# Graph attention with a routed feed-forward: output weights centred on chip, the second norm's variance from ScalarE, and side work dealt over the steps of a block

## The reference, cut

```python
def gnn(x, adj, Wq, bq, Wk, bk, Wv, bv, Wo, bo, gamma, beta):  # x: 8 x 1024 x 128, 4 heads of 32
    ...
    scores = clip(q @ k.T / sqrt(32), -10, 10)
    scores = where(adj == 0, -10, scores)
    attn = softmax(scores)             # for each chunk of 128 keys by itself
    out = sum_of_chunks(attn @ v) @ Wo.T + bo + x
    mu, var = mean(out), mean(square(out - mean(out)))
    return (out - mu) * rsqrt(var + 1e-5) * gamma + beta
def ffn(x, Wg, bg, W1, b1, W2, b2):     # 8 experts, hidden 256, the two best of each token
    mask = one_hot(top_k(x @ Wg + bg, 2)).sum()
    return sum_e(mask_e * (gelu(x @ W1_e + b1_e) @ W2_e + b2_e))
x = x + gnn(layernorm(x), adj, ...)     # layernorm has neither weight nor bias
x = x + ffn(layernorm(x), ...)
```

## Time and profile before

| | us |
|---|---|
| median of 3 runs | 757.75 (757.08 to 758.26) |
| span of the profiled execution | 773.1 |
| first clip of the loop / first clip of block 15 / last clip, by the trace | 17.08 / 504.8 / 541.95 |
| first clip of block 3 / of block 14 | 116.41 / 471.64 |
| clips of steps 2 and 3 of block 14 | 479.89, 484.11 |
| clips of steps 2 and 3 of block 15 | 514.68, 519.95 |
| TensorE / VectorE / ScalarE / GpSimd busy, of the span | 91% / 81% / 64% / 76% |

### The profile page before, as it was taken

How to read it: one execution, slowest core, us unless ns; L and a number is a source line. 1 busy time by engine, 2 the same in 40 slices (tenths; PEclk the granted TensorE clock), 3 DMA queues, 4 the chain that set the end, 5 groups by cost and what they waited for, 6 DMA issues and landing times. The chain is left out here.

```text
span 773.1 us, 17066 instructions
## 1 busy us (share of the span) xinstructions
PE 699.8 (91%) x5416; PEld 365.5 (47%) x5416; DVE 624.5 (81%) x1455; ACT 496.4 (64%) x898; POOL 584.0 (76%) x689
## 2 busy tenths in 40 slices
PE   4898999999999999999999999787979789999994
PEld 2222323333333333333333333231668679999994
DVE  4699899999999999999999999999677445545552
ACT  4656567777677775777767776544775346666663
POOL 7579495989879898798987988969476555667664
PEclk9999999999999999999999999997989789999998
DMA  7620000001010010100100001041322223333330
GB/s 272 212 65 28 12 18 14 28 29 56 15 43 28 29 56 15 43 28 29 56 15 29 29 15 43 15 138 42 88 68 75 81 81 94 88 86 98 100 90 1
DMA packets 47958, 45.42 MB, mean 59 GB/s; under 512 B 6981, under 2 KB 42576, under 8 KB 47872
## 3 DMA queue, kind: packets, MB, share of 16 engines
q1 hardware_dynamic: 41888, 31.60, 14.2%
q0 software_dynamic: 5984, 12.74, 4.5%
HBM read 27.73 MB, written 18.34 MB: 60 GB/s over the span
## 5 line engine op out<-in xcount | busy, mean ns | idle before, releaser
L744 ACT ACTIVATE e<-e 128x2048 f32<-128x2048 f32 x128 | 244.5, 1910 | 139.5 <-DVE e L946 132.6
L946 DVE SCALAR_TENSOR_TENSOR e<-scores_ps,bound_mem 128x2048 f32<-128x2048 f32 x128 | 292.2, 2283 | 25.6 <-PE scores_ps L436 23.8
L829 ACT ACTIVATE e<-scores_ps,bound_mem 128x128 f32<-128x128 f32 x364 | 104.4, 374 | 59.9 <-PE scores_ps L604 51.9
L1417 POOL DMA_INDIRECT out<-e,near x91 | 91.3, 1003 | 65.5 <-POOL near L1410 28.3
L455 PE MATMUL z_ps<-e,one_column 128*32 128x512 f32 x1024 | 136.0, 603 | 0.0
L1390 POOL TENSOR_TENSOR ctx_part<-ctx_part,z_inv 128x1024 f32<-128x1024 f32 x60 | 115.0, 1917 | 23.3 <-DVE z_inv L962 22.7
L1402 POOL TENSOR_TENSOR ctx_sum<-ctx_sum,ctx_part 128x512 f32<-128x512 f32 x90 | 115.8, 1287 | 6.0
L604 PE MATMUL scores_ps<-e,bound_mem 128*128 128x128 f32 x728 | 101.9, 284 | 8.7 <-ACT e L829 3.5
L604 PEld LDWEIGHTS scores_ps<-e,bound_mem 128*128 128x128 f32 x728 | 92.4, 198 | 12.0 <-issue 7.2
L954 DVE STREAM_TRANSPOSE ctx_part<-ctx_ps 128x512 f32<-128x512 f32 x128 | 90.3, 705 | 1.4 <-PE ctx_ps L448 1.3
L1364 POOL DMA_INDIRECT sorted_rows<-x_rows,slot x64 | 63.6, 994 | 27.2 <-issue 17.7
(11 more groups left out here) (171 smaller groups left out, 1032.1 us busy)
## 6 DMA issues: line engine op xcount, KB each, us to landing
near<-sorted_rows SPq DMA_DIRECT2D x91, 130.0 KB
near<-in_x SPq DMA_DIRECT2D x16, 256.0 KB, 2.7
bound_mem<-in_adjT SPq DMA_DIRECT2D x4, 1024.0 KB, 9.1
x_post<-in_x SPq DMA_DIRECT2D x16, 256.0 KB, 2.7
sorted_rows<-pad_row SPq DMA_DIRECT2D x1, 3640.0 KB, 14.7
out<-e,near POOLq DMA_INDIRECT x91
sorted_rows<-x_rows,slot POOLq DMA_INDIRECT x64
bound_mem<-in_w SPq DMA_DIRECT2D x1, 1024.0 KB
```

Source lines behind the costliest of these rows:

```text
L744: nc.scalar.activation(every, every, ACT.Exp, scale=SCORE_SCALE).then_inc(exp_done, 1)
L829: nc.scalar.activation(e_flat[:, h_at:h_at + P], scores_ps[:, i % 2, k * P:(k + 1) * P], ACT.Gelu, bias=part_flat[:, bias_at:bias_at + 1]) ...
L946: dve.scalar_tensor_tensor(out=e[:, s % E_RING], in0=scores_ps[:], scalar=-CLIP, in1=to, op0=ALU.max, op1=ALU.min).then_inc(clipped, 1)
L1417: nc.gpsimd.indirect_dma_start(out=out_rows, out_offset=bass.IndirectOffsetOnAxis(ap=near_u[:, id_at:id_at + 1], axis=0), in_=e_flat[:, at ...
```

## The change

The output weights are centred along the output features on chip: TensorE multiplies `Wo` by `centre` = I - 1/128, ScalarE copies the product to `wo_centred`, and the bias is centred likewise. The normalised x has mean zero already, so the projected sum has mean zero, and its variance is the mean of its squares. `statistics(ln["2"])` leaves VectorE, and `root(ln["2"])` GpSimd. Instead ScalarE squares the bank in `square_proj` with a sum as a second output, GpSimd makes the inverse root in `root_proj`, and ScalarE scales in `normalise_proj`. The projection is split in two halves over steps 1 and 2. `choose` is cut in three (`find_best`, `find_places`, `mark_pair`) for steps 2, 3 and 4, and the first norm's statistics begin with one tile in step 1. `mark_pair` writes its code to `job_ps[1]` for blocks under 11, after the wait for `n2_ready`. The wait of `turn_xn` on `one_hot_ready` becomes one on `gate_drained`. `normalise_x2` goes from step 6 to step 7, ahead of `drain_q`; GpSimd's `add_residual` goes ahead of `scale(u - 1, 4)`.

```diff
             def turn_xn(v):
-                need(pe, one_hot_ready, done(v - 5))
+                need(pe, gate_drained, done(v - 5))
...
-                    ins = pe.matmul(job_ps[1][:, cols], ctxT[:, cols], w_proj[:, W_O, :], start=False, stop=True,
+                    ins = pe.matmul(job_ps[1][:, cols], ctxT[:, cols], wo_centred[:], start=False, stop=True,
...
-            pe.matmul(job_ps[1][:, 0:1], w_proj[:, W_O, :], bv_sb[:], start=True, stop=True).then_inc(bias_filled, 1)
+            pe.wait_ge(centre_ready, 1)
+            pe.matmul(z_ps[:, 0:D], w_proj[:, W_O, :], centre[:], start=True, stop=True).then_inc(wo_filled, 1)
+            pe.wait_ge(wo_ready, 1)
+            pe.wait_ge(bv_ready, 1)
+            pe.matmul(z_ps[:, D:D + 1], wo_centred[:], bv_all[:], start=True, stop=False)
+            pe.matmul(z_ps[:, D:D + 1], centre[:], bo_sb[:], start=False, stop=True).then_inc(bias_filled, 1)
...
-                    if u < LATE and j == 2 and is_block(u - 2):
-                        project(u - 2)
-                    if u >= LATE and j in (1, 2):
+                    if j in (1, 2) and is_block(u - 2):
                         project(u - 2, range(2 * j - 2, 2 * j))
...
+            def square_proj(v):
+                need(act, x2_ready, v)
+                need(act, var2_ready, v)
+                act.wait_ge(proj_filled, v + 1)
+                for t in range(TILES):
+                    ins = nc.scalar.activation(n2[:, t, :], proj_rows[:, t, :], ACT.Square, scale=1.0 / float(np.sqrt(D)),
+                                               accum_out=mean_square[:, t, :])
+                ins.then_inc(squared, 1)
+
             def normalise_proj(v):
-                need(act, x2_ready, v)
-                normalise(ln["2"], v, n2, job_ps[1][:].rearrange("p (t d) -> p t d", d=D))
+                act.wait_ge(rstd2_ready, v + 1)
+                for t in range(TILES):
+                    ins = nc.scalar.activation(n2[:, t, :], proj_rows[:, t, :], ACT.Copy, scale=rstd2[:, t, :])
+                ins.then_inc(n2_ready, 1)
...
+            nc.scalar.activation(bv_all[:], bv_sb[:], ACT.Copy, scale=float(CHUNKS)).then_inc(bv_ready, 1)
+            act.wait_ge(wo_filled, 1)
+            nc.scalar.activation(wo_centred[:], z_ps[:, 0:D], ACT.Copy).then_inc(wo_ready, 1)
             normalise_x(0)
+            act.wait_ge(bias_filled, 1)
+            nc.scalar.activation(bo_all[:], z_ps[:, D:D + 1], ACT.Copy).then_inc(bias_ready, 1)
...
+                    if j == (7 if u < LATE else 6) and is_block(u - 2):
+                        normalise_x2(u - 2)
                     if j == 7 and u > 0 and is_block(u + 2):
                         drain_q(u + 2)
-                    if j == 6 and is_block(u - 2):
-                        normalise_x2(u - 2)
...
+            def mark_pair(v):
                 dve.wait_ge(best_at_ready, v + 1)
-                code = job_ps[0][:, 2 * P:2 * P + TILES].rearrange("p (t a) -> p t a", a=1)
+                if code_ps(v) is job_ps[1]:
+                    dve.wait_ge(n2_ready, v + 2)
+                code = code_ps(v)[:, 2 * P:2 * P + TILES].rearrange("p (t a) -> p t a", a=1)
...
+            def root_proj(v):
+                pool.wait_ge(squared, v + 1)
+                nc.gpsimd.tensor_scalar(var2[:], mean_square[:], 1.0, LN_EPS, ALU.mult, ALU.add).then_inc(var2_ready, 1)
+                pool.wait_ge(var2_ready, v + 1)
+                need(pool, n2_ready, v)
+                nc.gpsimd.tensor_tensor(rstd2[:], var2[:], minus_half[:, 0:TILES], ALU.pow).then_inc(rstd2_ready, 1)
...
-                if u >= LATE:
-                    root(ln["2"], u - 2)
+                if is_block(u - 2):
+                    root_proj(u - 2)
...
-                if k == 3:
-                    dve.wait_ge(proj_filled, 15)
-                    statistics(ln["2"], 14, proj_rows)
...
-                if k == 13:
-                    dve.wait_ge(proj_filled, 16)
-                    statistics(ln["2"], 15, proj_rows)
```

More of the change, by code:

```diff
@@ L519, in rank @@
                 if rank_ps(v) is job_ps[1]:
-                    need(pe, ln["2"]["s_out"], done(v if v == 13 else v + 1))
+                    need(pe, n2_ready, done(v if v == 13 else v + 1))
                 to = rank_ps(v)[:, 0:(TILES + 1) * NP].rearrange("p (t n) -> p t n", n=NP)
@@ L1010, in choose @@
                                   code_table[:].to_broadcast([P, TILES, NP]), ALU.is_equal).then_inc(one_hot_ready, 1)
+            def choose(v):
+                find_best(v)
+                find_places(v)
+                mark_pair(v)
             def place(v):
@@ new lines, in _ @@
+                    if u < LATE and is_block(u - 3):
+                        if j == 2:
+                            find_best(u - 3)
+                        if j == 3:
+                            find_places(u - 3)
+                        if j == 4:
+                            mark_pair(u - 3)
+                    if u >= LATE and j == (3 if u == LATE else 0):
+                        choose(u - 3)
+                    if j == 4 and is_block(u + 3):
+                        begin_statistics_x(u + 3, range(1 if u else 0, TILES))
@@ L1184, in _ @@
+                    if j == 5 and is_block(u - 2):
+                        begin_statistics_x2(u - 2)
+                        if u >= LATE:
+                            end_statistics(ln["3"], u - 2)
+                    if j == 6 and is_block(u + 3):
                         end_statistics(ln["1"], u + 3)
-                    if j == (6 if u < LATE else 5) and is_block(u - 2):
-                        dve.wait_ge(x2_ready, u - 1)
-                        statistics(ln["3"], u - 2, x_rows[:, (u - 2) % 3, :, D:2 * D])
+                    if j == 6 and u < LATE and is_block(u - 2):
+                        end_statistics(ln["3"], u - 2)
```

114 lines of the change are left out of this document (61 added, 53 removed).

## The result

The changed kernel takes 749.06 us (median of 4 runs, 746.87 to 752.06) where the kernel before, run beside it, takes 758.0 (757.08 to 759.22): a ratio of 0.9878, 95% interval 0.9854 to 0.9902. The forecast was 748.0 with a range of 743.5 to 756.

What follows compares the result with a forecast made beforehand. TensorE and VectorE, both nearly full, were taken to hold each other up in turn. Inner blocks -9.0, block 14 -0.3, block 15 -1.3, start +0.4, slots +0.5 gave -9.7: 748.0 us, range 743.5 to 756.

Steps and rivals of the forecast that it cites:

- What bounds the block: Inner block of 32.27 us: TensorE and VectorE alternate, heavy in different steps, so a block costs more than the fuller needs.
- The inner blocks: Blocks 3 to 13: longest of loop, VectorE and TensorE per step gives 31.45 against 32.27, 9.0 us in 11 blocks.
- step 0: Inner blocks: TensorE's turn waits for the normalisation moved behind step 7's exponential, losing 0.22 us, for 3.84.
- The squares: ScalarE, second norm: free up to 0.49 us each, beyond that 0.1 costs 0.4 a block; 0.42 assumed.
- (a): Squares cost 0.5 to 0.7 each, mark_pair holds step 5's clip; at 0.6 total 754; 0.17 shared with the slots rival.
- (b): Squares of 0.85 by a read-out emptying ScalarE each time: blocks 33.0, total 765, slower than before; chance 0.07.
- The start: Before the main loop: centring delays the first clip from 17.08 to 18.3, mostly hidden, +0.4 us (0.2 to 1.3).
- Blocks 14 and 15: Last blocks lose statistics in step 2: -0.3 and -1.3 us; step 4 of block 15 may move 2 us either way.
- After the last clip: Slots: VectorE loses two statistics of 1.4 us, ScalarE gains squares; +0.5 us, from -3 to +4.
- Rival (c): Slots, paced by ScalarE, give the gain back by +4 to +7: 752 to 755; 0.17 shared with (a).
- Rival (d): More gain: no turn_xn2 wait, block 15's port waits gone, half-clock stretches shrink: 743 to 746; chance 0.10.
- Carrying the microseconds over: Sum made in a profiled execution of 773.1 us, applied unscaled to the median of 757.75, giving 748.0.

Runs made afterwards that it cites:

- spare work in steps 7 and 3: The change plus four unread VectorE statistics a block in blocks 3 to 13: in step 7 748.13 us (blocks 31.40), in step 3 753.67 us (31.70).
- the deal: The kernel before with side work spread over steps as in the change, second norm's statistics left on VectorE: 768.47 us, ratio 1.0121.
- the norm without the deal: The change with projection and choose whole in step 2 again, keeping centred weights and squares on ScalarE: 752.89 us, ratio 0.9932.
- effective 0.75: The change with ScalarE's four squares and sums taken three times, extras unread: 765.1 us against 755.62 for the kernel before beside it.
- the second set: The change, unedited, run and profiled again beside other kernels on the same chip: 746.53 us, ratio 0.9852 to the kernel before.

## Why the prediction was right, point by point

**What bounds the block.** Right. The two engines held each other up in turn, and the statement that a block cost more than its fuller engine needs is what the change cashed in: TensorE's idle time went from 0.98 us a block to 0.19 (0.35 predicted). The spare work in steps 7 and 3 shows the same from the other side: free in one, 0.29 us in the other.

**The inner blocks.** Predicted 3.84, 4.67, 3.66, 3.62, 4.06, 3.62, 7.98, together 31.45; measured 3.71, 4.63, 3.74, 3.63, 4.06, 3.62, 8.00, together 31.39, where 9.0 us of gain were predicted and 9.9 came (355.23 to 345.35). The largest miss is step 0: the turn on TensorE was to lose 0.22 us waiting for the moved normalisation. It starts at 247.09, right behind the end of the normalisation at 247.04, and the row sums ahead of it end at 246.96: it waits about 0.1. The deal of step 2 into steps 3 and 4, and the keys that show in step 4, came as worked out. The same reckoning gave 32.11 and 33.0 for the norm and the deal done apart, and 32.12 and 33.02 were measured.

**The squares.** The threshold was right (0.49 predicted, 0.46 to 0.47 measured), and its slope too. Their price was not: 0.42 was taken, 0.25 measured. The bound of 0.46 rested on reading out the sum as an operation of its own, which it is, with 0.19 us near the 0.21 of the smallest activation. But it overlaps the activation before it and the one behind it, so that the pair takes no longer than one gelu does with its bias. By the page on activations (the Trainium skill, ScalarE: Activation LUTs, What ACT_TABLE_LOAD costs) the activation alone was 0.29; the row has 0.26. Since both prices lie under the threshold, the error cost the forecast nothing; it only made the rivals (a) and (b), with 0.5 to 0.7 and 0.85 as a price, look nearer than they were. Their blocks, at 0.6 and 0.85, were also a little off by the prediction's own slope, which gives 31.89 and 32.89 for 32.0 and 33.0. At an effective 0.75 a block takes 32.55, where the prediction's slope gives 31.45 + 4 (0.75 - 0.49) = 32.49, and the kernel does come out slower than before, so the mechanism of (b) is real.

**The start.** This is the term that was mis-sized: "+0.4 (0.2 to 1.3)". The part ahead of the first clip was as said, 17.08 to 18.21 where 18.3 was predicted, and as said it is mostly hidden: the norm without the deal has it too and reaches block 2 at 85.64. What was left out is another edit of the same diff: VectorE ends the statistics of block u + 3 in step 6 instead of 5, and in block 0 GpSimd stands in its queue for just that, with the bounds of block 1 behind it. That costs 1.0 us in step 7 of block 0, and taking this one line back gives it back. Block 1 is longer too, 33.27 and 33.26 before against 33.6 at the least with the change's start, and the granted clock falls there whenever the bound comes late. Both were put at nothing. Together they are 1.3 us or more, set by the order. With the line taken back the clock stays up, but block 1 takes 33.83, so what is left of its length isn't settled. A late load and a clock fallen in block 0 come on top, in kernels with and without the change alike: 85.3 to 87.4 before and 85.3 to 90.5 after at block 2. One profiled execution of each could not have told the true cost of the start to a microsecond.

**Blocks 14 and 15.** -0.3 and -1.3 predicted; -0.7 and -1.4 measured against the first execution. Step 2 of block 15 got 1.7 us shorter (5.27 to 3.56) where 1.39 were counted, and step 4 0.5 longer (8.86 to 9.37).

**After the last clip.** +0.5 (-3 to +4) predicted; 213.3 before, 212.9 and 213.7 after. Rival (c) did not come: statistics off VectorE and squares onto ScalarE leave the length as it was; that the two cancel is likely, but no run parts them. Rival (d), 743 to 746, was nearly reached in the second set, 746.53, with 0.9 us more from the inner blocks and more from the last ones than the forecast had. Of (d)'s three causes the wait of `turn_xn2` did come out smaller (0.1 us), and the second execution had no half-clock stretch in block 0, but step 4 of block 15 grew instead of shrinking.

**Carrying the microseconds over.** The sum was made in an execution 15 us longer than the median, and taken over unscaled. That came out right, for the excess lay behind the last clip (231.2 against 213.3) and not in the loop whose blocks were counted. The prediction gave no such reason, so this was in part luck. In that execution the granted clock was 0.85 between 575 and 633 us and 0.95 from there to the end; why it fell there isn't known. The whole was helped by luck too: the forecast of -9.7 met -8.9 because the inner blocks and the last ones gave 1.4 us more than counted and the start took more back.

## What to carry to other kernels

When two engines hand the bound back and forth, add up each step's work by engine, not each engine's total: taking 1.39 us off VectorE saved 0.17 us a block, spreading the side work alone cost 0.73, and both together saved 0.90. For every instruction that a diff moves by a step inside a loop, ask also what it does in the first and last turns, where another engine may stand in its queue for it. A spare copy of the disputed work, put in twice and three times, measures the threshold on which a forecast rests in two runs.

## What the runs showed of the hardware

An activation of 128x128 out of PSUM with a sum takes an ACTIVATE of 0.26 us and an ACTIVATION_READ_ACCUMULATOR of 0.19, and the pairs follow each other every 0.25 us. One VectorE sum of 128x640 took 0.78 us in one kernel and 1.79 in another; where it was the short one, it had started first and GpSimd's sum took 1.86 instead of 1.28. A load issued at 8.5 to 9.6 us behind 4 MB of adjacency landed between 20.3 and 22.4 us without regard to its issue; put ahead of half of the adjacency it was issued at 8.46, no earlier than in the kernel before, and was there before 19.3: here what stood ahead of it in the queue counted, not when it was issued. Contexts of three heads, each with 32 output columns, took as long as those of four. Behind a wait of TensorE of 2.13 us at the start of block 1 the granted clock fell within that block in nine executions of nine; in the five where it waited 1.14 us or less there, it did not. It is no rule for every wait: in block 0 of the change, again, TensorE waited 2.67 us and the clock stayed at 1.00.
